# A shared expert's 64-row tail: low part stacked beside the high part, two projection passes for three

## The reference

```python
x = x + jnp.tanh(g_xattn[0]) * xattn(_layernorm(x), ctx, ...)
xf = _layernorm(x).reshape(-1, 256)
...
s1 = xf @ shared_fc1.T            # 704 inner units
s2 = xf @ shared_fc2.T
shared = jax.nn.silu(s1) * s2 @ shared_proj.T
y = y + jax.nn.sigmoid(xf @ shared_gate_w.T) * shared
x = x + jnp.tanh(g_ffn[0]) * y
```

## Time and profile before

| what | value |
|---|---|
| median of 3 runs | 347.84 us (345.87 to 348.39) |
| the profiled execution | 347.91 us |
| its span, first to last instruction | 346.0 us |
| mean granted clock of TensorE | 0.950 |
| PE busy | 290.1 us (84%) |
| DVE (VectorE) busy | 222.5 us (64%) |
| ACT (ScalarE) busy | 156.2 us (45%) |
| POOL (GpSimd) busy | 115.7 us (33%) |

### The profile page before, as it was taken

One profiled execution on the slowest core, in us unless ns is written; L12 is line 12 of the kernel. 1 busy time (PEld: TensorE's weight loads), 2 busy tenths in 40 slices (PEclk: granted clock), 3 DMA queues, 4 the chain that ended last, 5 costly groups with the idle time before them and its releaser, 6 DMA issues.

```text
span 346.0 us, 5771 instructions
## 1 busy us (share of the span) xinstructions
PE 290.1 (84%) x1783; PEld 255.2 (74%) x1783; DVE 222.5 (64%) x716; ACT 156.2 (45%) x368; POOL 115.7 (33%) x123
## 2 busy tenths in 40 slices
PE   0688699869969974986999877999999998899992
PEld 0568578748847953674888766999999996788881
DVE  3647738697796577188466665777777772434356
ACT  1536525636633641332434524666666662332330
POOL 1401421251394087536300001454445443320500
PEclk9999989999998999598899969999999999999997
DMA  7620304115044017314556647343444421690006
GB/s 243 221 110 2 115 24 171 56 69 185 32 144 142 1 66 259 123 50 138 164 175 233 197 156 246 111 142 125 142 144 128 136 84 48 209 293 0 0 6 238
DMA packets 24605, 44.36 MB, mean 128 GB/s; under 512 B 2976, under 2 KB 17568, under 8 KB 24576
## 3 DMA queue, kind: packets, MB, share of 16 engines
q1 hardware_dynamic: 20736, 34.25, 30.6%
q0 software_dynamic: 3408, 9.57, 7.7%
q10 hardware_dynamic: 432, 0.18, 0.2%
HBM read 27.92 MB, written 16.06 MB: 127 GB/s over the span
## 4 chain that ended last, share of the span: by engine, by line
PE 59%; DVE 23%; DMA 6%; ACT 5%; issue 5%; SPq 1%; POOL 1%; DVEq 0%; ACTq 0%; POOLq 0%
PE bank L389 45%; PE bank L554 8%; DVE ew_lo L816 5%; PE bank L629 2%; PE bank L595 2%; DMA weight_stage<-wa_dram 2%; DVE ln_stats L863 2%; DVE work L859 2%; ACT ew_hi L652 2%; DVE work L1083 2%; DMA work<-xs_d 1%; DVE xn_all L1076 1%; DMA work<-x_dram 1%; ACT sh_hi L652 1%; DVE xn_all L874 1%
## 5 line engine op out<-in xcount | busy, mean ns | idle before, releaser
L389 PE MATMUL bank<-ew_hi 128*128 128x256 f32 (+1 forms) x164 | 54.7, 333 | 23.9 <-ACT ew_hi L652 14.7
L1217 POOL DMA_INDIRECT y_d<-work,dest_of_slot x39 | 37.5, 962 | 89.2 <-ACT work L652 71.4
L389 PE MATMUL bank<-ew_lo,ew_hi 128*128 128x256 f32 (+1 forms) x164 | 52.3, 319 | 5.3 <-DVE ew_lo L816 4.8
L389 PE MATMUL bank<-ew_hi,xt_hi 128*128 (+1 forms) x156 | 54.4, 349 | 1.1 <-DVE xt_lo L816 0.6
L389 PEld LDWEIGHTS bank<-ew_hi 128*128 128x128 f32 x164 | 32.2, 196 | 30.7 <-ACT ew_hi L652 13.9
L389 PE MATMUL bank<-ew_hi,ew_lo 128*128 128x256 f32 (+1 forms) x164 | 52.3, 319 | 0.0
L389 PE MATMUL bank<-ew_lo,xt_hi 128*128 (+1 forms) x156 | 47.9, 307 | 0.0
L652 ACT ACTIVATE ew_hi<-bank 128x512 fp32r<-128x512 f32 (+1 forms) x57 | 29.5, 537 | 39.9 <-PE bank L389 24.5
L816 DVE TENSOR_TENSOR xt_lo<-bank,xt_hi 128x256 fp32r<-128x256 f32 (+2 forms) x86 | 32.8, 385 | 15.3 <-ACT xt_hi L652 13.3
L652 ACT ACTIVATE xt_hi<-bank 128x256 fp32r<-128x256 f32 (+1 forms) x86 | 34.0, 402 | 16.7 <-issue 8.7
L816 DVE TENSOR_TENSOR ew_lo<-bank,ew_hi 128x512 fp32r<-128x512 f32 (+1 forms) x49 | 28.3, 597 | 18.9 <-ACT ew_hi L652 17.0
(11 more groups left out here) (128 smaller groups left out, 607.5 us busy)
## 6 DMA issues: line engine op xcount, KB each, us to landing
work<-xs_d SPq DMA_DIRECT2D x39, 136.0 KB
weight_stage<-ew_dram SPq DMA_DIRECT2D x10, 486.5 KB
work<-x_dram SPq DMA_DIRECT2D x8, 512.0 KB, 4.0
ew_hi<-y_d SPq DMA_DIRECT2D x8, 512.0 KB, 7.3
weight_stage<-sw_dram SPq DMA_DIRECT2D x4, 544.0 KB, 3.7
work<-ctx_t_dram SPq DMA_DIRECT2D x4, 512.0 KB, 5.6
x_d<-work SPq DMA_DIRECT2D x4, 512.0 KB
out_dram<-xn_all SPq DMA_DIRECT2D x3, 512.0 KB, 3.0
```

What stands on the lines that cost most here:

```text
L389: last = nc.tensor.matmul(dst, a, b, start=(n == 0), stop=(n == len(pairs) - 1))
L1217: nc.gpsimd.indirect_dma_start(out=y2_d, out_offset=bass.IndirectOffsetOnAxis(ap=IX[:, n:n + 1], axis=0), in_=EY[:, n % 4, :], in_offset=N ...
```

## The change

In block 5 VectorE writes the low part not into `SH[1]` but onto partitions 64 to 127 of `SH[0]`, beside the high part. The host fills rows 64 to 127 of block 5's projection weights with a copy of rows 0 to 63. The projection of block 5 then has two passes for each token tile: high part (64 rows) by the low weights, and high and low part stacked (128 rows) by the high weights. The wait for the low part stands at the second pass. Blocks 0 to 4 are as before.

```diff
             def pj(s, j):
-                rows = P if j < S_FULL else S_REST
+                full = j < S_FULL
+                if full:
+                    parts = [(SH[a][:, j % 2, :], SPJ[b][:, j, :]) for a, b in THREE]
+                else:
+                    parts = [(SH[0][0:S_REST, j % 2, :], SPJ[1][0:S_REST, j, :]), (SH[0][:, j % 2, :], SPJ[0][:, j, :])]
                 for t in range(TPC):
-                    for n, (a, b) in enumerate(THREE):
+                    for n, (h, w) in enumerate(parts):
                         if t == 0 and n == 0:
                             pe.wait_ge(a_hh, 6 * s + j + 1)
-                        if t == 0 and n == 2:
+                        if t == 0 and n == len(parts) - 1:
                             pe.wait_ge(v_hl, 6 * s + j + 1)
                         if j == 0 and n == 0 and s > 0:
                             pe.wait_ge(v_z, 4 * s - 3 + t)
-                        last = nc.tensor.matmul(B[4 + t][:, 0:D], SH[a][0:rows, j % 2, t * P:(t + 1) * P],
-                                                SPJ[b][0:rows, j, :], start=(j == 0 and n == 0),
-                                                stop=(j == S_FULL and n == len(THREE) - 1))
+                        last = nc.tensor.matmul(B[4 + t][:, 0:D], h[:, t * P:(t + 1) * P], w,
+                                                start=(j == 0 and n == 0), stop=(not full and n == len(parts) - 1))
                 last.then_inc(p_pj, 1)
...
                 dve.wait_ge(a_hh, 6 * s + j + 1)
-                sub(SH[1][0:rows, j % 2, :], SHF[0:rows, j % 2, :], SH[0][0:rows, j % 2, :]).then_inc(v_hl, 1)
+                lo = SH[1][:, j % 2, :] if j < S_FULL else SH[0][S_REST:2 * S_REST, j % 2, :]
+                sub(lo, SHF[0:rows, j % 2, :], SH[0][0:rows, j % 2, :]).then_inc(v_hl, 1)
...
     spj = np.zeros((S_BLK * P, D), f)
     spj[:F_S] = a["L0_ffn_shared_proj"].T
+    spj[F_S:] = spj[F_S - S_REST:F_S]
```

## The result

The changed kernel took 353.14 us (median), the kernel before 347.41 in the same series: ratio 1.0168, interval [1.0112, 1.0225]. Two more series of the changed kernel gave 1.0118 [1.0052, 1.0184] and 1.0161 [1.0105, 1.0217]. It is slower, by 1.2 to 1.7%, 4 to 6 us. Forecast were +2.2 us and 350.1, in a range up to 351.8. The direction was right and the change of height costs what the forecast said; the size was short by some 2 to 3.5 us.

A forecast was written before the change was run, and what follows sets the result against it. The prediction took TensorE (PE) to bound the kernel around block 5 of chunks 0 and 2. 0.66 + 0.78 + 0.66 + 0.09 = +2.19 us on 347.91 gave 350.1 us, range 348.0 to 351.8.

The forecast's parts named there:

- Six more changes at 0.19 and four passes fewer: Block 5 of chunks 0 and 2: +1.14 for height changes, -0.48 for saved passes, +0.66 us each.
- The first rival: Alternation in chunks 0, 1 and 2: height changes are free, only the pass count matters; -1.2 us, 346.7; chance 0.10.
- the second, half an overlap: Height changes in block 5: half of each is overlapped, 0.10 us a change; +0.57 us, 348.5; chance 0.10.
- The estimate worked out from the Trainium skill: Alternating 256-column passes: (398 + columns) / 2.4 ns, 0.272 us each, 0.15 over a hidden one; sum +1.47, 349.4.
- the +0.09 of the forecast: Chunk 3's end: VectorE's combine no longer starts before the end of the low part written from partition 64; +0.09 us, once.
- Chunk 3's passes stayed covered: Chunk 3's block 5: seven passes end at about 340.6, before VectorE's sums at 341.86; covered by 1.2 us.
- the term of chunk 1: Chunk 1's block 5 behind the low part: three passes fewer -0.36, six height changes +1.14; +0.78 us, nothing covering it.
- third rival: PE's clock falls to 1.2 GHz behind the alternation; +2.0 us, in two places +4.0, 354.1; chance 0.06.
- the stretch from 198 to 201 at 1.00: Argument against the clock falling: with PE idle for a third in 198 to 201, the granted clock was still 1.00.
- the delay is carried on: Behind chunk 0's block 5: work keeps its old order, so the 0.66 us delay reaches chunk 1's block 5.
- 0.38 us of cover: Chunk 2: VectorE's sums start at 317.91, the last pass ends at 316.87; 0.66 more stays covered, by 0.38.
- +0.66 up to chunk 1's low part: Chunk 0's block 5: the alternation's net cost of +0.66 us, carried on to chunk 1's block 5.

The follow-up runs named there:

- e2: The changed kernel with block 5's four 64-row passes first, then the four of 128 rows; against the kernel before 0.9998.
- e1: The changed kernel with block 5's first pass also on all 128 rows, so no 64-row pass; against the kernel before 0.9964.
- e4: The kernel before with the third of three passes per token tile on 128 rows, no stacking; against the kernel before 1.0159.
- both sets of fillers: Unread PE passes added to the changed kernel: 10 before chunk 1's block 5, 18 before chunk 2's first projection; against the kernel before 1.0062.
- e3: The kernel before with block 5's three passes all on 128 rows, no pass saved; against the kernel before 1.0076, then 1.0021.

## Why the prediction was right or wrong

**Right: the passes and the changes of height.** Six more changes at 0.19 and four passes fewer: +0.70 measured in chunk 2 for +0.66. e2 (order alone), e1 (no change of height) and e4 (changes without stacking) each show it by itself. The first rival, that passes alone count, falls with 0.31 at every change; the second, half an overlap, with it. The estimate worked out from the Trainium skill, TensorE: Matmul & The Clock Gate, section Single matmul latency, of 0.272 us for a pass that hides nothing is under the measured 0.31.

**Right: the small things.** VectorE's combine behind the low part, which writes from partition 64, no longer starts before its end. The timeline of DVE at the end, which answers to the earlier trace rows:

```profile
341.23 0.69 DVE L819 TENSOR_TENSOR sh_hi<-work,sh_hi 64x512 fp32r<-64x512 f32 x1 [0.69 <-ACT sh_hi L655]
341.94 3.50 DVE L1079 TENSOR_TENSOR xn_all<-xn_all,ew_hi 128x1024 f32<-128x1024 f32 x3
```

From start to start 0.71 for 0.61, +0.10 for the +0.09 of the forecast. Chunk 3's passes stayed covered, and VectorE still ends the run.

**Wrong: the term of chunk 1, "+6 x 0.19 = +1.14. Sum +0.78".** It measured +1.53 in the first trace: seven passes in 2.99 us (2.90 and 3.49 in the other two), 0.7 to 1.3 over the 2.2 of the sum. The failed step: it took full clock for passes that end later than any that the trace of before had there. I had the clock as third rival, but put it behind the alternation in chunks 0 and 2, where it stayed at 1.00, and weighed it with the stretch from 198 to 201 at 1.00. That stretch ends where the clock falls: from 201 to 203 it was 0.72. A longer block 5 reached into it.

**Wrong: "Everything behind is fc passes with their silu, product and copies in the old order, so the delay is carried on."** In chunk 3 the delayed low part met an operation that was not delayed: GpSimd's adds start behind chunk 2's sums, and I had shown myself, 0.38 us of cover in the earlier trace rows, that the sums don't move. So the low part moved against the adds by 0.7 us and was held, 2.48 us in place of 0.81; +0.42 to +0.44 at the end, which the forecast had at nothing.

**Small: +0.82 for +0.66 up to chunk 1's low part.** ScalarE's copy of a weight piece waits for its DMA there, since SP takes up the piece only when the store of chunk 0's sums has landed (6.3 us after its issue in this trace, 5.1 before). It is no chance of one trace: SP went on 6.4 to 6.6 us behind the issue in all three traces of the changed kernel, and 5.1 and 5.4 in the two of the kernel before. Why the store is longer was not tried.

**Open.** 2.19 and these terms make 3.4 to 4.0 us by the traces; the three series give 4.1 to 5.8. The traces show the quicker executions: 351.58, 350.54 and 351.18 us, each some 1.5 us under the median of its series, all at a mean granted clock of 0.943. Over the executions behind the ratios the mean is 0.939, 0.940 and 0.939 for the changed kernel, and 0.948 in the second and third series for the kernel before; with both sets of fillers the changed kernel has 0.949. All executions of the changed kernel up to 352.0 us had 0.942 or more, and all the longer ones 0.939 or less. So the rest goes with the lower clock too. In which stages it fell in the longer ones, and whether that is the cause of all they lost, is not shown, since none was traced.

The +1.05 behind the experts is not shown to be the change's. Of the 13 traces without the fillers there, ten run part of chunk 2's first projection and fc at the lower clock (5.8 to 7.4 us for both in place of 4.7), among them e1 and both of e3, in which no height changes; the first trace of the kernel before, e2, and e4, which alternates, do not. None of the seven with those fillers does. What this costs does not show in the medians: the kernel before came out with fillers as without them (0.9997).

## What to carry to other kernels

Count the changes between passes of 64 rows and of 128 rows, not only the passes: each cost 0.19 us here, more than the 0.119 of a pass saved. A stacked operand cost nothing here when the passes beside it had 112 or 128 rows, and little when passes of one height stood together (e2: 1.33 us for eight passes, two changes of height). When work is made longer at the end of a stage, read the stretch right behind it too, for the clock and for other engines' operations that do not move along.

## What was not expected of the hardware

Changes of height at every pass cost the sum of both single parts, 0.31 us from start to start for 256 columns at 2.4 GHz, and 0.51 at the lower clock (1.2 GHz). VectorE's subtraction of two SBUF inputs waited 1.8 us for a GpSimd add with SBUF inputs, while its product with a PSUM input did not. Twenty-eight passes whose results nobody reads, in time in which PE was idle anyway, took the changed kernel's median from 352 to 353 us down to 350.15, and left the kernel before where it was (0.9997).
